# A vision tower on one core: moving three slot products, two exponentials and two variances in the first stage

## What is computed

```python
h = tok(x)                               # 16x16 patches -> 143 tokens + cls, D = 128
h = h + attn0(layernorm(h))              # in-proj, causal conv of 4 taps, gated linear scan, out-proj
h = h + ffn0(layernorm(h))               # branch below
h = h + attn1(layernorm(h))              # windowed attention, 8 heads
h = h + ffn1(layernorm(h))               # one of 16 experts per image
```

## Time and profile before

| what | us |
| --- | --- |
| median of three runs | 2887.75 |
| lowest and highest | 2885.34 and 2888.98 |
| the profiled execution, its own time | 2891.1 |
| its span from first to last instruction | 2888.0 |
| busy: TensorE, VectorE, ScalarE, GpSimd | 2576.3, 2083.3, 1803.9, 1033.2 |

### The profile page before, as it was taken

One profiled execution on the slowest core, in us unless ns is written; L12 is line 12 of the kernel. 1 busy time (PEld: TensorE's weight loads), 2 busy tenths in 40 slices (PEclk: granted clock), 3 DMA queues, 4 the chain that ended last, 5 costly groups with the idle time before them and its releaser, 6 DMA issues.

```text
span 2888.0 us, 71290 instructions
## 1 busy us (share of the span) xinstructions
PE 2576.3 (89%) x25177; PEld 2032.2 (70%) x25177; DVE 2083.3 (72%) x6017; ACT 1803.9 (62%) x3853; POOL 1033.2 (36%) x916
## 2 busy tenths in 40 slices
PE   6998999999898988499999997899999999999996
PEld 4666666666666665399999996676677776667765
DVE  3788888888888888455555554577777777777775
ACT  3777767767777776344444443566766676666674
POOL 1355555555555555455555554101110111000100
PEclk9999999999999999699999998999999999999998
DMA  3222222222222211377777775121112211122110
GB/s 136 70 83 84 85 83 82 83 83 89 87 98 84 87 60 35 107 233 229 228 235 228 228 233 171 39 67 51 51 51 61 65 51 51 51 62 62 51 34 29
DMA packets 135788, 288.40 MB, mean 100 GB/s; under 512 B 22752, under 2 KB 79072, under 8 KB 131424
## 3 DMA queue, kind: packets, MB, share of 16 engines
q1 hardware_dynamic: 113504, 245.36, 27.9%
q0 software_dynamic: 22016, 39.43, 4.2%
HBM read 215.79 MB, written 68.92 MB: 99 GB/s over the span
## 4 chain that ended last, share of the span: by engine, by line
PE 62%; DVE 20%; ACT 12%; issue 4%; DMA 1%; POOL 1%; SPq 0%; DVEq 0%; ACTq 0%; POOLq 0%
PE psum L513 15%; PE psum L1190 9%; PE psum L1181 9%; PE psum L519 4%; PE psum L1592 3%; PE psum L1535 3%; PE psum L1552 3%; ACT nrows L1752 3%; PE psum L1540 2%; ACT ex L1788 2%; DVE acc L816 2%; PE psum L1605 2%; PE psum L1575 2%; ACT r L1758 2%; ACT r L1760 2%
## 5 line engine op out<-in xcount | busy, mean ns | idle before, releaser
L1225 ACT ACTIVATE hid<-psum,w_blk 128x256 f32<-128x256 f32 x608 | 268.9, 473 | 325.0 <-PE psum L1181 325.0
L1047 POOL DMA_INDIRECT expert_in<-rows,slot_i x384 | 376.7, 981 | 157.0 <-issue 140.6
L1788 ACT ACTIVATE ex<-psum,smin 128x80 f32<-128x80 f32 x1152 | 281.1, 331 | 206.9 <-DVE smin L1874 206.8
L1153 POOL DMA_INDIRECT expert_out<-rows_out,dest x304 | 291.0, 957 | 290.5 <-DVE rows_out L1320 242.3
L513 PE MATMUL psum<-xn,w_in 128*128 128x288 f32 x1024 | 313.5, 432 | 31.6 <-ACT rf L726 27.6
L1190 PE MATMUL psum<-w_blk,hid 128*128 128x128 f32 x2432 | 297.2, 276 | 0.0
L1181 PE MATMUL psum<-x_t,w_blk 128*128 128x256 f32 x1216 | 289.6, 382 | 2.2 <-DMA w_blk<-w_exp_in 2.2
L1190 PEld LDWEIGHTS psum<-w_blk,hid 128*128 128x128 f32 x2432 | 284.4, 193 | 0.1
L1514 POOL TENSOR_TENSOR x2c<-x2c,ycho 96x768 f32<-96x768 f32 x32 | 57.7, 1802 | 611.4 <-DMA ycho<-expert_out 611.4
L513 PEld LDWEIGHTS psum<-xn,w_in 128*128 128x128 f32 x1024 | 192.0, 200 | 99.3 <-DVE xn L874 40.4
L1017 POOL TENSOR_TENSOR unit<-unit 128x576 f32<-128x576 f32 x64 | 120.0, 1875 | 354.9 <-ACT unit L680 272.7
(11 more groups left out here) (259 smaller groups left out, 5789.8 us busy)
## 6 DMA issues: line engine op xcount, KB each, us to landing
w_blk<-w_exp_in SPq DMA_DIRECT2D x152, 578.5 KB
xin<-x_in SPq DMA_DIRECT2D x32, 1716.0 KB, 7.1
rows_in<-expert_in SPq DMA_DIRECT2D x152, 132.0 KB
ycho<-expert_out SPq DMA_DIRECT2D x64, 288.0 KB, 5.3
h_dram<-h SPq DMA_DIRECT2D x32, 288.0 KB, 2.1
x_dram<-rows SPq DMA_DIRECT2D x32, 288.0 KB, 3.2
h1c<-h_dram SPq DMA_DIRECT2D x32, 288.0 KB, 4.4
x2c<-x_dram SPq DMA_DIRECT2D x32, 288.0 KB, 5.2
```

Of the source, the lines that this page charges most:

```text
L1047: pool.indirect_dma_start(out=expert_in[:, :], out_offset=bass.IndirectOffsetOnAxis(ap=slot_i[z.s][:, n:n + 1], axis=0), in_=rows[z.s][:, ...
L1153: pool.indirect_dma_start(out=expert_out[:, :], out_offset=bass.IndirectOffsetOnAxis(ap=dest[b.s][:, c:c + 1], axis=0), in_=rows_out[b.s][ ...
L1225: nc.scalar.activation(hid[b.s][:, c, :], HB[b.s][c % HK], ACT.Gelu_apprx_tanh, bias=w_blk[b.q][:, FF + FC * D + c:FF + FC * D + c + 1]).t ...
L1788: done = nc.scalar.activation(ex[u][:, b, in_window(qb)], score_bank(u)[:, b * QK:(b + 1) * QK], ACT.Exp, bias=smin[u % RING][:, b:b + 1], ...
```

## The change

Three things are edited, all in the first stage's lists.

- TensorE: the three slot products move from behind unit 4 to the end of the step, behind variance 2. DVE's ranks, weights and cast move with them, to the end of its step.
- ACT: the two Exp of layernorm 0 move ahead of the mixer's Square, and the branch's Square ahead of the mixer's Ln.
- Banks and buffers: the mixer's variance goes to A0 instead of B0 and waits for the second `normed`; unit 0, which uses B0, no longer waits for the mixer's Ln; the branch's variance stays in A0 and waits for that Ln instead. The branch's Square writes `sq` instead of `sqf`, its Ln and Exp use `ra` instead of `rf`, and ACT's wait for `x2_step` goes.

```diff
                 if z:
                     pe.wait_ge(squared3, z.upto(1, 1))
-                    project(B0, C("mean"), sqf[:]).then_inc(variance3, 1)
+                    if x:
+                        pe.wait_ge(normed, x.upto(2, 2))
+                    project(A0, C("mean"), sqf[:]).then_inc(variance3, 1)
                 if x:
                     pe.wait_ge(normed, x.upto(2, 1))
-                    if z:
-                        pe.wait_ge(logvar3, z.upto(1, 1))
                     unit_in(x, 0, B0)
                 if y:
                     pe.wait_ge(squared1, y.upto(1, 1))
                     if x:
                         pe.wait_ge(normed, x.upto(2, 2))
-                    project(A0, C("mean"), sqf[:]).then_inc(variance1, 1)
+                    if z:
+                        pe.wait_ge(logvar3, z.upto(1, 1))
+                    project(A0, C("mean"), sq[:]).then_inc(variance1, 1)
...
                     unit_in(x, 4, B0)
-                if z:
-                    if x:
-                        pe.wait_ge(unit_act, x.upto(8, 4))
-                    ranks(z, A1)
                 if x:
...
                     project(B0, C("mean"), sqf[:]).then_inc(variance2, 1)
+                if z:
+                    if x:
+                        pe.wait_ge(unit_act, x.upto(8, 4))
+                    ranks(z, A1)
...
-                if z:
-                    act.wait_ge(centered3, z.upto(1, 1))
-                    nc.scalar.activation(two(sqf[:]), both(A1), ACT.Square, bias=shift1[:, 0:1]).then_inc(squared3, 1)
                 if x:
                     act.wait_ge(logvar0, x.upto(2, 1))
                     nc.scalar.activation(rb[:], rb[:], ACT.Exp, scale=-0.5).then_inc(rstd0, 1)
                     act.wait_ge(logvar0, x.upto(2, 2))
                     nc.scalar.activation(ra[:], ra[:], ACT.Exp, scale=-0.5).then_inc(rstd0, 1)
                 if z:
+                    act.wait_ge(centered3, z.upto(1, 1))
+                    nc.scalar.activation(two(sqf[:]), both(A1), ACT.Square, bias=shift1[:, 0:1]).then_inc(squared3, 1)
+                if y:
+                    act.wait_ge(centered1, y.upto(1, 1))
+                    nc.scalar.activation(two(sq[:]), both(B1), ACT.Square).then_inc(squared1, 1)
+                if z:
                     act.wait_ge(variance3, z.upto(1, 1))
-                    nc.scalar.activation(two(rf[:]), both(B0), ACT.Ln, bias=eps_col[:, 0:1]).then_inc(logvar3, 1)
-                if y:
-                    act.wait_ge(centered1, y.upto(1, 1))
-                    nc.scalar.activation(two(sqf[:]), both(B1), ACT.Square).then_inc(squared1, 1)
+                    nc.scalar.activation(two(rf[:]), both(A0), ACT.Ln, bias=eps_col[:, 0:1]).then_inc(logvar3, 1)
...
                     act.wait_ge(variance1, y.upto(1, 1))
-                    if z:
-                        act.wait_ge(x2_step, z.upto(2, 1))
-                    nc.scalar.activation(two(rf[:]), both(A0), ACT.Ln, bias=eps_col[:, 0:1]).then_inc(logvar1, 1)
+                    nc.scalar.activation(two(ra[:]), both(A0), ACT.Ln, bias=eps_col[:, 0:1]).then_inc(logvar1, 1)
                     act.wait_ge(logvar1, y.upto(1, 1))
-                    nc.scalar.activation(rf[:], rf[:], ACT.Exp, scale=-0.5).then_inc(rstd1, 1)
+                    nc.scalar.activation(ra[:], ra[:], ACT.Exp, scale=-0.5).then_inc(rstd1, 1)
...
                     delta(x, 1)
-                if z:
-                    route_ranks(v, z, A1)
                 if x:
                     tap(x, 1, 2)
-                if z:
-                    route_slots(v, z)
                 if y:
...
                 if z:
+                    route_ranks(v, z, A1)
                     route_weights(v, z)
+                    route_slots(v, z)
```

More of the change, by code:

```diff
@@ L724, in step @@
                 if z:
-                    act.wait_ge(variance3, z.upto(1, 1))
-                    nc.scalar.activation(two(rf[:]), both(B0), ACT.Ln, bias=eps_col[:, 0:1]).then_inc(logvar3, 1)
+                    act.wait_ge(centered3, z.upto(1, 1))
+                    nc.scalar.activation(two(sqf[:]), both(A1), ACT.Square, bias=shift1[:, 0:1]).then_inc(squared3, 1)
                 if y:
                     act.wait_ge(centered1, y.upto(1, 1))
-                    nc.scalar.activation(two(sqf[:]), both(B1), ACT.Square).then_inc(squared1, 1)
+                    nc.scalar.activation(two(sq[:]), both(B1), ACT.Square).then_inc(squared1, 1)
+                if z:
+                    act.wait_ge(variance3, z.upto(1, 1))
+                    nc.scalar.activation(two(rf[:]), both(A0), ACT.Ln, bias=eps_col[:, 0:1]).then_inc(logvar3, 1)
                 if z:
@@ L883, in step @@
                     v.wait_ge(rstd1, y.upto(1, 1))
-                    v.tensor_tensor(two(x0[:]), both(B1), two(rf[:]), ALU.mult).then_inc(pool_step, 1)
+                    v.tensor_tensor(two(x0[:]), both(B1), two(ra[:]), ALU.mult).then_inc(pool_step, 1)
                     v.wait_ge(pool_step, y.upto(3, 1))
```

## The result

| what | before, us | after, us |
| --- | --- | --- |
| median (four runs each) | 2887.68 | 2906.59 |
| lowest and highest | 2885.34 and 2888.98 | 2904.01 and 2910.59 |
| span of the profiled execution | 2888.0 | 2902.0 |
| L884 to L884, mean of 31 intervals | 34.96 | 35.71 |

The ratio is 1.0068, with a 95% interval of 1.005 to 1.0085: slower by 0.7%, where 2872 was forecast, and outside the range. The last row is the cleaner measure of the first stage: the time from the last x0 product to the end of the span, which lies nearly all in the two stages that no run edits, is between 1719 and 1741 us in the profiled executions of all the kernels here. 35.71 − 34.96 = 0.75 a step, 23 us over the stage.

A forecast was written before the change was run, and what follows sets the result against it. Bound: a loop of 26.87 us full DVE plus 7.99 through ACT and TensorE. 6.99 + 12.65 + 14.70 = 34.34 against 34.86; over 30 intervals −15.6, and 2891.1 − 15.6 − 3.35 = 2872 us, range 2838 to 2897.

The forecast's parts named there:

- Path, 6.99: From the mixer's last add through ACT and TensorE to L884: 7.99 us a step before, forecast to fall to 6.99.
- Part 3, 14.70: From x1 to the mixer's end: 12.99 us before, forecast 14.70 with ranks and cast moved in.
- the held time: DVE's ranks held beside POOL's two products, about 1.1 us each, 2.2 a step, replacing 1.72; called the softest term.
- Part 2, 12.65: From L884 to x1 (L929): 13.88 us before, forecast 12.65, as the moved ranks and cast leave (−1.23).
- about 1.05 of the 1.35 held there goes: Comparison L954 on DVE, held by POOL's residual add, would lose 1.05 us of hold, which becomes a wait before x1.
- The clock, nothing in the sum: TensorE's lower granted clock after an idle gap: 1.7 us lost per 3.4 us of work, taken as costing little.
- the figure of 0.1: Average cost a step of the low clock before the change: mean period 34.96 us against 34.86.
- the 0.35 of slack: TensorE's margin before the mixer's add: out-projection ends at 517.10, centring starts at 517.44; called a bare 0.35 us.
- The gap itself: TensorE's idle wait, now ending at variance 2: forecast about 1.9 us instead of 2.26.
- the forecast's 34.34: Forecast step from one L884 to the next in the first stage: 34.34 us against 34.86, a gain of 0.52.
- the one that put the bound on TensorE: Rival: low clock makes the out-projection 1.2 us late in half the steps; 2888 within 3 us, chance 0.22.
- The slower one: Rival: POOL holds two rank multiplications and the weights' product, 3.1 to 3.7 us a step; say 2905, chance 0.13.

The follow-up runs named there:

- e1: The change without its moves of TensorE's slot products and DVE's ranks and cast, so only new banks and ACT order; 2881.68 us, 0.9971 of before.
- e3: The changed kernel plus three spare column halves of unit 4's product on TensorE ahead of variance 2; 2889.07 us, 0.9994 of before.
- e12: The changed kernel with six of POOL's twelve scatters put behind its residual add in the next step, no spare products; 2878.87 us, 0.9950 of before.
- e4: The kernel before the change plus three spare column halves of unit 4's product on TensorE ahead of the slot products; 2887.93 us, 0.9991 of before.
- e9: The changed kernel plus three spare column halves ahead of variance 2, and six of POOL's twelve scatters behind its next residual add; 2868.31 us, 0.9933 of before.
- e2: The kernel before the change with only the moves of slot products and DVE's ranks and cast, on old banks and ACT order; 2904.88 us, 1.0054.

## Why the prediction was wrong

**Path, 6.99.** Right: 7.07, 0.08 more. The branch's variance follows the mixer's Ln directly, and the exponentials fit ahead of the mixer's Square; both hold in e1 and in after.

**Part 3, 14.70.** Right, 14.69 (835.12 to 849.81), and the held time with it: 2.18 for 2.2. Two of the ranks' instructions are held, but the first is the count L989, not a rank multiplication (L996 in before, L994 in after), and the second is held by POOL's add (L1031), which the prediction counted as a product; the weights' product L1009 is free (0.17). The Trainium skill (SBUF — State Buffer, its section SBUF: two separate sides) says that the two engines exclude each other for the whole instruction, whichever starts first. L989 at 1.31 for 0.16 and L959 at 1.92 for 0.19 agree that they exclude each other, but the order doesn't: L959 starts at 859.32 and POOL's add at 859.74, and it is L959 that waits.

**Part 2, 12.65.** Right in an undisturbed step (12.57), wrong in most. The step that failed is "the add falls mostly beside work ahead of L954, and about 1.05 of the 1.35 held there goes". That POOL would scatter 1.7 earlier was right (20.03 for 21.74). But the twelve then took 859.74 − 842.58 = 17.16, where 527.37 − 512.26 = 15.11 was read before (the add after those of the earlier trace rows). The second scatter, now beside the start of the scan, took 3.33. With 15.11 the add would have started 0.81 after L884, and ended 2.23 after it, just past L952's start, so that little would have been held, as forecast. It starts at 2.86, spares L952 and holds L959 for 1.92 instead. I counted the start of the queue, not how long what stands in it takes under other neighbours. No run has the moved ranks without the long scatter, so the 0.81 stays a sum on paper. In e1 the add comes as late (2.85) without a long scatter: there the scatters start later (22.30 after L884) and the next L884 comes sooner. The price of the hold, with the clock at 1.00, is 34.94 − 34.32 = 0.62 a step.

**The clock, nothing in the sum.** Failed as well: 0.77 a step with the hold in place (e3), 0.38 without it (e12). The two can't be ranked, as the 0.39 between these figures belongs to hold and clock together. For before the figure of 0.1 was near (e4: 0.18). What I took from before was the price of a low stretch there, 3.4 us beside work with slack. After the change x1 has lost its cover, so the same stretch lands on variance 2 and makes x1 wait, and from there through unit 6 and the embedding on the out-projection, with the 0.35 of slack that I had named. The gap itself was forecast at 1.9 and is 1.77; in the held steps it is 2.18 to 2.39.

So 34.32 + 0.62 + 0.77 = 35.71, as measured. Both prices are differences between these runs, so that this sum closes by itself; what is a test is that the first figure, that of e9 with both causes gone, is the forecast's 34.34.

**The rivals:** the one that put the bound on TensorE, at 0.22, has part of the clock's mechanism, the out-projection that comes late in half of the steps (17 waits of 1.0), but these waits grew by 5.2 us only; the waits for x1's root, which it didn't name, grew by 14.1. The slower one came near the time (2905) by luck, for another reason: it wanted held ranks of more than 2.7 a step, and these stayed at 2.18; POOL's collision is in the next step, with its residual add. That most of what the shorter path saves goes again while POOL holds DVE was in none.

## What to carry to other kernels

When a path in a loop gets shorter, ask of every engine outside it where its queue now ends against the new start of the step, and cost the queue to its last instruction. Work ahead of a wait is its cover: moving 1.2 us of small instructions behind a waiting one saved nothing here, and makes the wait as sensitive as the chain behind it. Where a stream of products has one gap of about 2 us a step, try spare products in it before pricing anything else: with them the stages can be compared without the clock.

## What the runs showed of the hardware

A scatter that began 0.14 after the second scan of `y` (843.88; the scan started at 843.74) ran until the end of the third instruction behind it (847.21), 3.33 instead of 0.92. All of POOL's 384 in after took 436.4 us, before 376.7. Scatters of over 2 us stand, 29 in each, in exactly the six kernels with DVE's half of the move; the other eight have none. In after one that began 0.88 behind the scan still took 2.57, to the same end; in before and e1 one that began 0.94 behind it took 1.2, and the next, beside the second and third of those instructions, 1.01. What makes the difference isn't settled. The Trainium skill (SBUF — State Buffer, its box on DVE blocking DMA) says that DVE can keep GpSimd from writing a transfer's descriptors; it tells it of another kind of DVE instruction, and no run here takes the case apart.

Three spare column halves a step held the granted clock at 1.00 from 150 to 1130 us (e3, e4), and in the kernel before they cost nothing that could be measured (0.9991, 0.998 to 1.0003). What makes a low stretch last about 6.8 us in 9 places of after and 3.4 elsewhere stayed open. The length of the one gap doesn't settle it: five of the nine begin in steps where variance 2 waited 1.77 (the one at 221.9 us, for instance), four behind a wait of 2.3 to 2.4 (that of the rows above), and five steps with a wait of 2.2 to 2.35 have no low stretch at all. With the hold gone (e12) none of 6.8 is left between 140 and 1100 us, yet e2, with L954 held in every full step, has none there either. By which way the hold brings them is not shown.
